# A fused two-layer block on one core: the second layer's gated perceptron multiplies in half-precision pieces

## The reference, cut to what matters

```
h   = silu(x @ W_up[e].T + b_up[e]) * (x @ W_gate[e].T + b_gate[e])      # 256 hidden
out = h @ W_down[e].T + b_down[e]
```

## Time and profile before

| | |
|---|---|
| median of 3 runs | 495.83 us (495.53 to 496.1) |
| the profiled execution, its own time | 493.75 us |
| its span in the trace | 492.0 us |
| PE busy | 442.2 us, 90% |
| DVE busy | 404.4 us, 82% |
| ACT busy | 234.5 us, 48% |

### The profile page before, as it was taken

One profiled execution on the slowest core, in us unless ns is written; L12 is line 12 of the kernel. 1 busy time (PEld: TensorE's weight loads), 2 busy tenths in 40 slices (PEclk: granted clock), 3 DMA queues, 4 the chain that ended last, 5 costly groups with the idle time before them and its releaser, 6 DMA issues.

```text
span 492.0 us, 9511 instructions
## 1 busy us (share of the span) xinstructions
PE 442.2 (90%) x3723; PEld 308.4 (63%) x3723; DVE 404.4 (82%) x906; ACT 234.5 (48%) x426; POOL 54.5 (11%) x69
## 2 busy tenths in 40 slices
PE   7999999998899989302899999999999999999997
PEld 6446999987358754100289896667666665666676
DVE  6997789787797659999834689987898999999786
ACT  5976555473842239894645554336324222423110
POOL 2005000000680005400081000000000000000000
PEclk9999999999999999755999998999999999999999
DMA  8879997950180004403330006455772000000000
GB/s 290 329 302 369 392 389 305 372 232 1 43 300 1 1 0 130 128 0 128 129 97 1 1 14 247 133 212 167 263 263 97 5 13 7 7 7 6 7 7 27
DMA packets 23475, 66.69 MB, mean 136 GB/s; under 512 B 2980, under 2 KB 5415, under 8 KB 23303
## 3 DMA queue, kind: packets, MB, share of 16 engines
q1 hardware_dynamic: 22992, 65.98, 37.3%
q10 hardware_dynamic: 438, 0.11, 0.1%
HBM read 38.68 MB, written 1.18 MB: 81 GB/s over the span
## 4 chain that ended last, share of the span: by engine, by line
PE 25%; DVE 25%; issue 4%; ACT 1%; DVEq 0%
PE bk L733 8%; DVE XT L1674 6%; DVE X L1662 4%; PE bk L741 4%; DVE RA L1702 4%; PE bk L778 3%; PE bk L661 2%; PE bk L615 2%; DVE RA L1494 1%; DVE WK L1528 1%; PE bk L753 1%; PE bk L624 1%; PE bk L631 1%; DVE QS L1402 1%; PE bk L652 1%
## 5 line engine op out<-in xcount | busy, mean ns | idle before, releaser
L733 PE MATMUL bk<-X,RB 128*128 128x512 f16 x384 | 94.6, 383 | 0.5 <-DVE X L1662 0.3
L1021 ACT ACTIVATE X<-RA 128x512 f16<-128x512 f32 x64 | 40.3, 630 | 100.3 <-DVE RA L1702 84.1
L1674 DVE SCALAR_TENSOR_TENSOR XT<-bk,WK,XT 128x128 f32<-128x128 f32 x192 | 67.0, 349 | 5.3
L733 PEld LDWEIGHTS bk<-X,RB 128*128 128x128 f16 x384 | 37.1, 99 | 42.1 <-DVE X L1662 1.5
L741 PEld LDWEIGHTS bk<-RB,X 128*128 128x128 f16 x768 | 48.5, 98 | 15.4 <-issue 0.6
L741 PE MATMUL bk<-RB,X 128*128 128x128 f16 x768 | 53.5, 219 | 0.0
L1662 DVE TENSOR_TENSOR X<-RA,X 128x512 f16<-128x512 f32 x64 | 43.8, 684 | 1.1 <-ACT X L1021 1.1
L874 ACT ACTIVATE WK<-bk 128x512 f32<-128x512 f32 x48 | 28.6, 595 | 28.9 <-PE bk L404 22.3
L778 PE MATMUL bk<-RB,RA 128*128 128x512 f16 x144 | 38.8, 379 | 0.9 <-DVE RA L1719 0.9
L1309 DVE SCALAR_TENSOR_TENSOR RB<-WK,WCOL,bk 128x512 f32<-128x512 f32 x32 | 23.7, 743 | 11.4 <-ACT WK L874 11.4
L404 PE MATMUL bk<-X,RC 128*128 128x128 f16 x480 | 29.7, 219 | 0.0
(11 more groups left out here) (327 smaller groups left out, 877.6 us busy)
## 6 DMA issues: line engine op xcount, KB each, us to landing
RC<-RA SPq DMA_DIRECT2D x20, 768.0 KB, 5.2
STG<-RA SPq DMA_DIRECT2D x8, 768.0 KB, 5.6
RC<-expert_weights SPq DMA_DIRECT2D x22, 256.0 KB, 6.4
RC<-in_wx SPq DMA_DIRECT2D x7, 768.0 KB, 7.3
X<-in_w SPq DMA_DIRECT2D x8, 512.0 KB, 3.6
RA<-RA SPq DMA_DIRECT2D x4, 768.0 KB, 5.0
RC<-in_w SPq DMA_DIRECT2D x8, 384.0 KB, 4.0
STG<-expert_weights SPq DMA_DIRECT2D x12, 256.0 KB, 6.3
```

Source lines behind the costliest of these rows:

```text
L733: t = e.matmul(BK[m][:, :], P16[:, wp, wo:wo + 128], ZH[:, n % 4, xp, :], start=(e1 == 0 and i == 0), stop=(e1 == 15 and i == 2))
L1021: e.activation(ZH[:, r, 0, :], zf[r], ACT.Copy).then_inc(S("z_hi"), 1)
L1674: stt(XT[:, bb_(t_)], bank_o(n)[:, bb_(i)], RW[:, t_, e1:e1 + 1], XT[:, bb_(t_)], ALU.mult, ALU.add).then_inc(S("acc"), 1)
```

## The change

The up and gate products of the perceptron take the three-pass form.

- The weights are split by `c2_hi(b)` on ACT and `c2_lo(b)` on DVE, 128 x 512 elements each, 16 times each. They stand in three places: for samples 12 to 15 and 4 to 7 in the end of layer 0's attention, for 0 to 3 in the feed-forward (ACT) and behind its end (DVE), for 8 to 11 within the perceptron.
- The f32 blocks of samples 12 to 15 and then of 4 to 7 arrive in the same four staging pieces `GU[b]` of `RC`. So each of these blocks becomes two transfers (512 columns and 256 columns), and the load of block 4, 5, 6, 7 waits for `c2_lo` of block 12, 13, 14, 15.
- `x4_hi(c)` (ACT) and `x4_lo(c)` (DVE) split the tokens of chunk c, 128 x 512 each, four times each. `mlp_up` waits for `x4_lo` in place of `x4`, and for `c2_lo`.
- The factor 256 is taken out again by a scale in ACT's silu and in `x5`, and by one small new DVE instruction for the gate's bias (`BSELW`).
- The transfers for 12 to 15 are issued before the half-swaps instead of behind them.

```diff
+        GU = {b: RC[:, 512 * (b % 4):512 * (b % 4) + 512] if b // 4 in (1, 3) else C2W[b][:, 0:512] for b in range(16)}
+        SPLIT_AT = {b: i for i, b in enumerate((12, 13, 14, 15, 4, 5, 6, 7, 0, 1, 2, 3, 8, 9, 10, 11))}
...
             def mlp_up(b):
-                q.wait_ge(f"c2w{b}", 16)
-                q.wait_ge("x4", b // 4 + 1)
+                q.wait_ge("c2_lo", SPLIT_AT[b] + 1)
+                q.wait_ge("x4_lo", b // 4 + 1)
                 q.wait_ge(*(("hid", 2 * (b - 1)) if b >= 2 else ("x2", 4)))
                 for i in range(4):
-                    t = e.matmul(BK[6 + b % 2][:, bb_(i)], C2W[b][:, bb_(i)], XT[:, bb_(b)], start=True, stop=True)
+                    for n, (wp, xp) in enumerate(PASSES):
+                        t = e.matmul(BK[6 + b % 2][:, bb_(i)], GU16[b][:, wp, bb_(i)], X4H[:, b // 4, xp, bb_(b % 4)], start=(n == 0), stop=(n == 2))
...
+            def c2_hi(b):
+                q.wait_ge(f"c2w{b}", 32 if b // 4 in (1, 3) else 16)
+                if b // 4 == 2:
+                    q.wait_ge("c2_lo", SPLIT_AT[b - 8] + 1)
+                e.activation(GU16[b][:, 0, :], GU[b], ACT.Copy, scale=WS).then_inc(S("c2_hi"), 1)
+
             for t2 in range(8):
+                if t2 >= 4:
+                    c2_hi(8 + t2)
                 q.wait_ge("vmm", t2 + 1)
...
+            for b in range(4, 8):
+                c2_hi(b)
             for o in range(8):
                 wbot(o)
...
+            def c2_lo(b):
+                q.wait_ge("c2_hi", SPLIT_AT[b] + 1)
+                stt(GU16[b][:, 1, :], GU[b], WS, GU16[b][:, 0, :], ALU.mult, ALU.subtract).then_inc(S("c2_lo"), 1)
+
+            for b in range(12, 15):
+                c2_lo(b)
             for i in range(3):
                 fw_lo(i)
...
             for c in range(4):
+                if c:
+                    c2_lo((15, 4, 5)[c - 1])
                 for ch in range(2):
...
+                if c < 2:
+                    c2_lo(6 + c)
                 stt(XT[:, cc(c)], BK[6 + c % 2][:, :], col("bo"), XT[:, cc(c)], ALU.add, ALU.add).then_inc(S("x1"), 1)
...
+            def chosen(b):
+                w = A["w1"][bass.ds(row[b, 0], 128), :]
+                if b // 4 in (1, 3):
+                    if b < 8:
+                        q.wait_ge("c2_lo", b - 3)
+                    e.dma_start(GU[b], w[:, 0:512]).then_inc(S(f"c2w{b}"), 16)
+                    e.dma_start(C2W[b][:, 512:768], w[:, 512:768]).then_inc(S(f"c2w{b}"), 16)
```

More of the change, by code:

```diff
@@ L69 @@
     (("x_lo", 4), ("xq", 4), ("quant", 12), ("ot_lo", 3)),
-    (("route", 29), ("router", 114), ("rw", 3), ("done", 4)),
+    (("route", 30), ("router", 114), ("rw", 3), ("done", 4)),
     (("chosen", 5), ("l1p", 1), ("relm", 1), ("cos", 32), ("p16", 8)),
@@ L165, in program @@
         BSEL = sb("BSEL", [128, 5, 16])
+        BSELW = sb("BSELW", [128, 2, 16])
         QS = sb("QS", [128, 64])
@@ L260, in program @@
         ROOT = 12
-        ROUTED, EXP_IN, WEIGHTS, BIASES = 13, 15, 24, 29
+        ROUTED, EXP_IN, WEIGHTS, BIASES = 13, 15, 24, 30
         PREP = {"bsc": 1, "kr": 2, "aw": 3, "th": 4, "sn": 5, "on3": 11, "bv": 14, "fq": 21}
@@ L312, in program @@
         C2W += [STG[:, i // 2, CE * (i % 2):CE * (i % 2) + CE] for i in range(4)] + [RC[:, CE * i:CE * i + CE] for i in range(8)]
+        GU = {b: RC[:, 512 * (b % 4):512 * (b % 4) + 512] if b // 4 in (1, 3) else C2W[b][:, 0:512] for b in range(16)}
+        GU16 = [QT[:, 512 * b:512 * b + 512] for b in range(4)] + [C2W[b][:, 0:512] for b in range(4, 8)]
+        GU16 += [C2W[b - 8][:, 0:512] for b in range(8, 12)] + [C2W[b][:, 0:512] for b in range(12, 16)]
+        GU16 = [w.bitcast(F16).rearrange("p (h n) -> p h n", h=2) for w in GU16]
+        SPLIT_AT = {b: i for i, b in enumerate((12, 13, 14, 15, 4, 5, 6, 7, 0, 1, 2, 3, 8, 9, 10, 11))}
+        X4H = big(5).bitcast(F16).rearrange("p (c h n) -> p c h n", c=4, h=2)
         X3, ZT, PT, VV = big(0), big(1), big(2), big(3)
@@ L972, in scalar @@
                     e.activation(G16[j][:, h], GT[j][:, h], ACT.Identity, scale=rq(3)).then_inc(S("gated16"), 1)
+            q.wait_ge("gated_ff", 5)
+            for b in range(4):
+                c2_hi(b)
             for j in range(3):
@@ L996, in su @@
                 for i in range(2):
-                    t = e.activation(SU[b % 3][:, bb_(i)], BK[6 + b % 2][:, bb_(i)], ACT.Silu, bias=BSEL[:, i, b:b + 1])
+                    t = e.activation(SU[b % 3][:, bb_(i)], BK[6 + b % 2][:, bb_(i)], ACT.Silu, bias=BSEL[:, i, b:b + 1], scale=1.0 / WS)
                 t.then_inc(S("su"), 1)
@@ L1003, in x5 @@
                     b = 4 * c + i
-                    t = e.activation(X5[:, bb_(b)], BK[4 + c % 2][:, bb_(i)], ACT.Identity, bias=BSEL[:, 4, b:b + 1])
+                    t = e.activation(X5[:, bb_(b)], BK[4 + c % 2][:, bb_(i)], ACT.Identity, bias=BSEL[:, 4, b:b + 1], scale=1.0 / WS)
                 t.then_inc(S("x5"), 1)
@@ L1021, in z_hi, with x4_hi @@
                 e.activation(ZH[:, r, 0, :], zf[r], ACT.Copy).then_inc(S("z_hi"), 1)
-            for job, n in ((x3, 0), (x3, 1), (z, 0), (vv, 0), (x3, 2), (z, 1), (x3, 3), (vv, 1), (z, 2), (vv, 2), (su, 0), (su, 1), (z, 3), (vv, 3),
-                           (su, 2), (su, 3), (su, 4)):
+            def x4_hi(c):
+                q.wait_ge("x4", c + 1)
+                e.activation(X4H[:, c, 0, :], XT[:, cc(c)], ACT.Copy).then_inc(S("x4_hi"), 1)
+            for job, n in ((x3, 0), (x3, 1), (z, 0), (vv, 0), (x3, 2), (z, 1), (x3, 3), (vv, 1), (x4_hi, 0), (z, 2), (vv, 2), (su, 0), (x4_hi, 1),
+                           (su, 1), (z, 3), (vv, 3), (c2_hi, 8), (x4_hi, 2), (su, 2), (c2_hi, 9), (su, 3), (c2_hi, 10), (x4_hi, 3), (su, 4), (c2_hi, 11)):
                 job(n)
@@ L1178, in routing @@
                     yield
+                then(route)
+                ts(BSELW[:, :, :], BSEL[:, 2:4, :], WS, None, ALU.mult).then_inc(route.next(), 1)
                 assert route.n == BIASES
+                yield
             def prep_lora():
@@ L1527, in hid @@
                 for i in range(2):
-                    stt(HG[b % 3][:, bb_(i)], BK[6 + b % 2][:, bb_(2 + i)], BSEL[:, 2 + i, b:b + 1], SU[b % 3][:, bb_(i)], ALU.add, ALU.mult).then_inc(S("hid"), 1)
+                    stt(HG[b % 3][:, bb_(i)], BK[6 + b % 2][:, bb_(2 + i)], BSELW[:, i, b:b + 1], SU[b % 3][:, bb_(i)], ALU.add, ALU.mult).then_inc(S("hid"), 1)
             rt = Steps(S, "router")
@@ L1634, in router, with x4_lo @@
                 yield
-            for job, n in ((pp, 0), (x4, 0), (pp, 1), (x4, 1), (pp, 2), (hid, 0), (x4, 2), (hid, 1), (pp, 3), (hid, 2), (x4, 3), (hid, 3)):
+            def x4_lo(c):
+                q.wait_ge("x4_hi", c + 1)
+                tt(X4H[:, c, 1, :], XT[:, cc(c)], X4H[:, c, 0, :], ALU.subtract).then_inc(S("x4_lo"), 1)
+            for b in range(4):
+                c2_lo(b)
+            for job, n in ((pp, 0), (x4, 0), (x4_lo, 0), (pp, 1), (x4, 1), (pp, 2), (hid, 0), (x4_lo, 1), (x4, 2), (hid, 1), (pp, 3), (c2_lo, 8),
+                           (x4_lo, 2), (hid, 2), (x4, 3), (c2_lo, 9), (hid, 3), (c2_lo, 10), (x4_lo, 3)):
                 job(n)
@@ L1647, in vector @@
                 hid(b)
+                if b == 4:
+                    c2_lo(11)
                 if b >= 6:
@@ L1840, in sync @@
                 fetch(u)
+            def chosen(b):
[5 more added lines that the diff above has]
+                    e.dma_start(C2W[b][:, 512:768], w[:, 512:768]).then_inc(S(f"c2w{b}"), 16)
+                else:
+                    e.dma_start(C2W[b], w).then_inc(S(f"c2w{b}"), 16)
+            q.wait_ge("down", UNITS)
+            for b in (12, 13, 14, 15):
+                chosen(b)
             for c in range(4):
@@ L1849, in halve @@
                 e.dma_start(XF[:, 1024 * (i % 2):1024 * (i % 2) + 1024], A["w2"][:, 1024 * i:1024 * i + 1024]).then_inc(S(f"w2_{i % 2}"), 16)
[L1851 to L1855, removed]
+            for b in (4, 5, 6, 7):
                 chosen(b)
```

## The result

| | before | changed |
|---|---|---|
| median | 495.72 us (4 runs, 495.53 to 496.1) | 503.68 us (4 runs, 498.81 to 504.52) |
| the profiled execution, its own time | 493.75 us | 503.86 us |
| its span | 492.0 us | 502.0 us |
| ratio of the changed kernel to before | | 1.0138, interval 1.0108 to 1.0169 |

The changed kernel takes 7.96 us more. The forecast was 500.0 (498.2 to 502.3): its sign was right, its size was half of what came. In a later series of six runs the median was 504.39 and the ratio 1.019 (1.0163 to 1.0216).

A forecast was written before the change was run, and what follows sets the result against it. PE was taken as the bound (busy 442.2 of 492.0 us), with DVE from 276 to 288 us. Slip 3.8 plus perceptron 0.4 gave 4.2 us on the median 495.83: 500.0 us, range 498.2 to 502.3.

The forecast's parts named there:

- The slip: End of layer 0's attention: ACT's first `wbot` copy waits for block 7, delaying PE to the end, 3.8 us.
- The landing: Block 7's two transfers, issued after `c2_lo(15)`, land 2.9 us after the first issue.
- The splits for 12 to 15 and the rest of 4 to 7: End of layer 0's attention: these splits fall into gaps and waits of ACT and DVE and cost nothing.
- `BSELW`: One instruction on 32 columns in the expert stage, where PE sets the pace: nothing, at most 0.2 us.
- Rival B: PE's clock falls in the new gap at the third `wbot` product: 1.5 us more, 501.5 us; chance 0.30.
- the row's gap: Trace row cited on the clock: after 4.75 us idle, one small PE product took 0.47 us.
- The splits for 0 to 3: ACT's four take 2.5 us of 9.97 idle, DVE's four 2.8 of 3.86 idle: nothing.
- The perceptron: 258 to 293 us: PE's shorter products against DVE's added splits, +0.4 us net (-1.5 to +1.5).
- The replay: DVE's perceptron order recomputed with row durations: `hid(2)` to `hid(5)` late, the router's first step 0.8 us late.

The follow-up runs named there:

- run 11: The changed kernel once more, unchanged, with six more runs: 504.39 us.
- run 1: Changed kernel with `c2_lo(15)` run earlier, with those of 12 to 14 ahead of `fw_lo`: 498.77 us, ratio to before 1.0065.
- run 7: Changed kernel with the earlier `c2_lo(15)`, plus `c2_lo(8..11)` writing one column and `mlp_up(8..11)` multiplying the high half twice: 496.69 us.
- Run 2: Changed kernel plus 15 unused f16 products on PE ahead of the third `wbot` product, to keep PE busy in the gap: 502.09 us.
- Run 4: Changed kernel with `c2_lo(0..3)` writing one column and `mlp_up(0..3)` multiplying the high half twice, POOL unmoved: 500.54 us.
- run 3: Changed kernel with POOL's second half of `p16` waiting for the last `x4_lo`: 508.91 us.
- run 5: Changed kernel with the earlier `c2_lo(15)`, plus POOL's second half of `p16` waiting for the first `pp`: 495.56 us, ratio to before 0.9996.
- run 6: Changed kernel with one edit alone, POOL's second half of `p16` waiting for the first `pp`: 500.79 us.
- run 9: Changed kernel with earlier `c2_lo(15)`, POOL making low halves of blocks 0 to 3, blocks 8 to 11 split right behind `x2`, `p16` behind them: 495.59 us.

## Why the prediction was right and wrong

*The slip, 3.8 us (3.1 to 4.6).* Right in place, mechanism and size: 3.62 measured (4.02 in run 11), and it goes with the one instruction named (run 1). The landing was taken as 2.9 us and took 3.0 from the first issue.

*The splits for 12 to 15 and the rest of 4 to 7, `BSELW`: nothing.* Right. Run 1 keeps them all, and 5.19 and 11.75 us stand against 5.20 and 11.71 before; the earliest start of `gmm` with the change is 157.94 us (run 7), before 157.97.

*Rival B, the clock, +1.5, chance 0.30.* It came, at 1.65 us. The price was right; the error was the chance. Against it I had set "that the row's gap is longer and that PE had done little just before it", but no row showed that either makes a difference. The Trainium skill, "TensorE: Matmul & The Clock Gate", Part 1, says that the default state is throttled and that activity releases the throttle. Run 2 agrees with it: with work in the gap the granted clock stays at 1.00. With B as the main case the forecast would have been 501.5, still 2.2 us short: the rest is the next term.

*The splits for 0 to 3: "Nothing".* **This is the step that failed.** "DVE's four take 2.8 us where it was idle 3.86" took the duration of a row (0.69) where DVE was alone, and counted DVE's idle time as free time. POOL was working at that place on two tensors in SBUF. In the kernel before, DVE's only work there read one of its tensors from a bank, so its trace showed no collision in this place. It did show one elsewhere, which I overlooked: a low half made beside a two-tensor instruction of POOL, ending 0.55 us behind it, took 1.28 us where most of the 36 of its line take 0.68.

```profile
36.24 2.86 POOL L1758 TENSOR_TENSOR RB<-RB 128x1024 f32<-128x1024 f32 x1 [26.14 <-DMA RB<-in_l1m]
38.37 1.28 DVE L1315 TENSOR_TENSOR RB<-RB 128x512 f16<-128x512 f32 x1
```

In the changed kernel the four took 6.7 us, and `x4_lo(0)` 2.65: `mlp_up(0)` came 2.88 us late. Run 4 (without these four) and runs 3, 5 and 6 (with POOL elsewhere) all bring back 12.56 us.

*The perceptron, +0.4 net (-1.5 to +1.5).* Right within its bounds: -0.15 in run 5 and +0.05 in run 6, where POOL is out of the way. The replay was pessimistic: it had the router's first step 0.8 us late, and in run 5 it came 30.84 us behind `x2`, against 30.78 before. As forecast, in the changed kernel `mlp_up(4)` to `(6)` wait for `hid` (0.53, 0.30 and 0.38 us), the twelve products take 0.67 us from start to start, and DVE gives away what PE saves. Run 7 shows the other side of it: without four of the splits the router starts 1.19 us earlier.

In sum: forecast 3.8 + 0.4 = 4.2; measured 3.62 + 1.65 + 2.72 = 7.99, with the last term 2.88 - 0.15. The difference of 3.8 is 1.65 (clock) + 2.88 (POOL) - 0.55 (perceptron, -0.15 for +0.4) - 0.18 (slip).

*Still open.* The one run of 498.81 fits none of the terms alone. Beyond the gap, the clock falls at changing places in several versions, for some 3.5 us in run 1 (from 291 us) and for 14 us in the profiles of runs 2 and 11 (303 to 317 and 305 to 318 us), where two executions of each took over 4 us more than the rest; whether the shorter f16 products or PE's new waits bring it about was not settled. The rule of the Trainium skill cited above says nothing of a fall under a busy PE, which run 11 shows. And no version beats the kernel before: the best, runs 5 and 9, are level with it.

## What to carry to other kernels

Idle time of an engine is room only for instructions that don't collide with what its neighbours do at that moment. Before placing a two-tensor DVE instruction in a gap, look at POOL's row of the same window, look through the whole trace for an instruction of the same form that ran beside POOL, and ask which of the operands lie in a bank; where they collide, delay the engine that isn't on the chain to a place where DVE works on banks or waits for PE, never onto a chain of small steps. And when an edit makes PE wait for some microseconds, count the gap and add the half-speed work behind it; a few useless products in the gap can be cheaper.

## What the runs showed of the hardware that I had not expected

- DVE with two tensors in SBUF stands until POOL's running instruction ends: the router's steps on four columns ended within 0.02 us of POOL's (0.16 us became 1.00 and 1.56), `x4_lo(0)` 0.54 us behind it (0.68 became 2.65). It goes the other way too: POOL's subtraction took 2.44 us instead of 2.13 beside `c2_lo`.
- POOL's same 13 us of work cost 2.9 us beside splits of 512 columns, and 10.0 us beside the router's steps of four columns (57.29 against 47.27 us from `x2` to the first `weighed`): there the chain stood again and again, and PE's clock was at half from 289 to 306 us, which is part of the 10.0.
- Not only instructions with two tensors stood: of the router's steps in run 3 two `TENSOR_SCALAR` (L1589 and L1602) took 1.40 and 0.95 us for 0.17, ending within 0.03 us of POOL's. `hid`, `pp` and `x4`, which take a tensor from a bank, kept theirs.
- 3.4 us of products with no use, in a gap of 3.7 us, gave 1.66 us back.
